# Softmax sums of a cross-attention block: from halves added by GpSimd to one VectorE reduction

## What is computed

```
q = (layernorm(x) @ Wq + bq)          # x: 8 x 1024 x 512, 16 heads of 32
k, v = ctx @ Wk + bk, ctx @ Wv + bv   # ctx: 8 x 64 x 384
attn = softmax(clip(q k^T / sqrt(32), -1e4, 1e4))    # over 64 keys
x = x + (attn @ v) @ Wo + bo
hidden = layernorm(x) @ W1 + b1       # 512 -> 2048
q = hidden + phase * w_imag * sin(theta + 0.1 hidden) * 0.1
out = x + relu(q) @ W2 + b2
```

## Time and profile before

| | |
|---|---|
| median of 3 runs | 1959.45 us (1958.43 to 1963.11) |
| the profiled execution | 1960.21 us, of which the traced span is 1958.1 us |
| TensorE matmul busy in the span | 1941.3 us, 99% |
| VectorE busy | 1486.9 us, 76% |
| ScalarE busy | 1263.7 us, 65% |
| GpSimd busy | 545.6 us, 28% |
| mean granted TensorE clock | 0.998 of full speed |

### The profile page before, as it was taken

One profiled execution on the slowest core, in us unless ns is written; L12 is line 12 of the kernel. 1 busy time (PEld: TensorE's weight loads), 2 busy tenths in 40 slices (PEclk: granted clock), 3 DMA queues, 4 the chain that ended last, 5 costly groups with the idle time before them and its releaser, 6 DMA issues.

```text
span 1958.1 us, 27917 instructions
## 1 busy us (share of the span) xinstructions
PE 1941.3 (99%) x9162; PEld 1624.4 (83%) x9162; DVE 1486.9 (76%) x2304; ACT 1263.7 (65%) x2132; POOL 545.6 (28%) x388
## 2 busy tenths in 40 slices
PE   9999999999999999999999999999999999999999
PEld 7788888888888878888888888888888888888887
DVE  8988888888875967787578768758757876875763
ACT  6767767667664867677377557647737755764761
POOL 7877777777773321000000000000000000000000
PEclk9999999999999999999999999999999999999999
DMA  7467687687675999889879888987987988897845
GB/s 243 145 185 185 172 209 179 172 214 190 169 157 161 339 323 336 277 271 290 275 264 270 265 280 252 286 289 238 290 272 266 270 267 279 252 286 245 250 151 193
DMA packets 363298, 472.75 MB, mean 241 GB/s; under 512 B 166032, under 2 KB 201872, under 8 KB 363152
## 3 DMA queue, kind: packets, MB, share of 16 engines
q1 hardware_dynamic: 346448, 439.44, 70.7%
q0 software_dynamic: 15840, 31.46, 9.4%
q10 hardware_dynamic: 864, 0.04, 0.0%
HBM read 347.90 MB, written 108.00 MB: 233 GB/s over the span
## 4 chain that ended last, share of the span: by engine, by line
PE 89%; DVE 4%; POOL 2%; DMA 2%; issue 2%; ACT 2%; SPq 0%; POOLq 0%; ACTq 0%; DVEq 0%
PE psum L1980 29%; PE psum L1982 29%; PE psum L1981 29%; PE psum L2073 2%; DMA stage<-in_w 1%; POOL prob L942 1%; PE psum L2022 0%; POOL prob L963 0%; DMA x_dram<-res 0%; DVE top L1617 0%; DMA acc<-in_w 0%; DVE prob L1608 0%; DVE stats L1481 0%; POOL q_lo L898 0%; DVE xt_lo L1717 0%
## 5 line engine op out<-in xcount | busy, mean ns | idle before, releaser
L1980 PE MATMUL psum<-w_ring,act_hi 128*128 128x512 f32 x1024 | 399.7, 390 | 3.6 <-DVE act_lo L1819 3.6
L1981 PE MATMUL psum<-w_ring,act_hi 128*128 128x512 f32 x1024 | 399.5, 390 | 0.0
L1982 PE MATMUL psum<-w_ring,act_lo 128*128 128x512 f32 x1024 | 399.5, 390 | 0.0
L1982 PE MATMUL psum<-xo,w_ring 128*128 128x512 f32 x784 | 305.1, 389 | 0.0
L1980 PE MATMUL psum<-xo,w_ring 128*128 128x512 f32 x784 | 305.1, 389 | 0.0
L1981 PE MATMUL psum<-xo,w_ring 128*128 128x512 f32 x784 | 305.1, 389 | 0.0
L1798 DVE SCALAR_TENSOR_TENSOR frac<-frac,turns 128x512 f32<-128x512 f32 x256 | 175.8, 696 | 77.3 <-ACT frac L1346 77.2
L1980 PEld LDWEIGHTS psum<-w_ring,act_hi 128*128 128x128 f32 x1024 | 192.8, 188 | 44.5 <-issue 4.4
L1982 PEld LDWEIGHTS psum<-w_ring,act_lo 128*128 128x128 f32 x1024 | 192.9, 188 | 40.1
L1981 PEld LDWEIGHTS psum<-w_ring,act_hi 128*128 128x128 f32 x1024 | 192.9, 188 | 39.9
L1383 ACT ACTIVATE frac<-frac 128x512 f32<-128x512 f32 x256 | 156.0, 626 | 104.4 <-DVE frac L1798 104.4
(11 more groups left out here) (186 smaller groups left out, 4341.1 us busy)
## 6 DMA issues: line engine op xcount, KB each, us to landing
w_ring<-w2s SPq DMA_DIRECT2D x240, 512.0 KB, 4.2
w_ring<-w1s SPq DMA_DIRECT2D x392, 256.0 KB, 4.2
x_sb<-turn_dram SPq DMA_DIRECT2D x58, 512.0 KB, 6.3
res<-in_x SPq DMA_DIRECT2D x64, 256.0 KB, 3.8
x_dram<-res SPq DMA_DIRECT2D x64, 256.0 KB, 3.1
x_dram<-bo_row POOLq DMA_DIRECT2D x16, 1024.0 KB, 11.0
acc<-x_dram SPq DMA_DIRECT2D x16, 1024.0 KB, 7.3
x_sb<-in_x SPq DMA_DIRECT2D x15, 1024.0 KB, 6.2
```

What stands on the lines that cost most here:

```text
L1980: pe.matmul(o, a_hi, b_hi, start=first, stop=False, skip_group_check=resumed)
L1981: pe.matmul(o, a_hi, b_lo, start=False, stop=False, skip_group_check=resumed)
L1982: return pe.matmul(o, a_lo, b_hi, start=False, stop=last, skip_group_check=resumed)
```

## The change

`total` of a group is now reduced by VectorE straight from the 64 exponentials of each head in `prob`: 128 partitions x 16 rows x 64 elements. Before, it reduced 128 x 16 x 32 elements of `halves`. GpSimd's addition that filled `halves` goes, with its two waits and its semaphore. VectorE waits for the exponential (`exp_done`) instead of the addition. The place of `sum_and_inverse` in each step's order is the same, as is all the rest.

```diff
             for i in range(GROUPS + 1):
-                if i:
-
-                    rows = prob[:, (i - 1) % SCORE_BUFS]
-                    pool.wait_ge(exp_done, i)
-                    if i >= 2:
-                        pool.wait_ge(total_done, i - 1)
-                    pool.tensor_tensor(halves[:], rows[:, :, 0:KEYS // 2], rows[:, :, KEYS // 2:KEYS], ALU.add)\
-                        .then_inc(halves_done, 1)
                 if i in V_LO_STEPS:
...
             def sum_and_inverse(i):
                 if 1 <= i <= GROUPS:
-                    dve.wait_ge(halves_done, i)
+                    dve.wait_ge(exp_done, i)
                     if i >= 3:
                         dve.wait_ge(prob_done, i - 2)
-                    dve.reduce_sum(total[:, (i - 1) % 2, :], halves[:], AX_X).then_inc(total_done, 1)
+                    dve.reduce_sum(total[:, (i - 1) % 2, :], prob[:, (i - 1) % SCORE_BUFS], AX_X).then_inc(total_done, 1)
```

More of the change, by code:

```diff
@@ L311, in xattn_ffn @@
         stats_raw, shift_rows_done = sem("stats_raw"), sem("shift_rows_done")
-        q_full_done, halves_done = sem("q_full_done"), sem("halves_done")
+        q_full_done = sem("q_full_done")
         xt_psum, xt_hi_done, xt_lo_done = sem("xt_psum"), sem("xt_hi_done"), sem("xt_lo_done")
```

## The result

The changed kernel takes 1963.88 us in the median of 20 runs (1961.0 to 1969.3), the kernel before 1960.55 us in the median of 20 runs beside it (1958.34 to 1963.11). The ratio is 1.0016, with a 95% interval of 1.0010 to 1.0022: 3.3 us or 0.16% slower, where 5.1 us were forecast. It lies within the 0.3% that the prediction calls no change, on the forecast side.

A forecast was written before the change was run, and what follows sets the result against it. TensorE was taken as the bound in settled attention, VectorE as pacing before about 97 us. Tiles +4.3, first tiles +1.5 and last groups -0.7 gave +5.1 us on 1959.45, about 1964.6 us; eight-in-ten range 1959.8 to 1969.0.

The forecast's parts named there:

- The place: Once per tile, a later `top` of group 29 delays `q_lo` of group 30 and TensorE, paid in full.
- Hidden everywhere: Rival: TensorE's prefetch and VectorE's idle time absorb the 0.38 us delay; about 1960.3 us, chance 0.12.
- The size of that term: Per settled tile, two longer sums less the vanished wait for `halves`: +0.38 us, in eleven tiles.
- Step 57: Its wait for `halves` is longer, 1.00 us, so the change costs only 0.1 us there.
- The first tiles: Up to 97 us VectorE sets the pace; longer sums, partly relieved, cost TensorE +1.5 us, bounds -0.5 to +2.9.
- `rstd`, which was queued behind it, moves into its place for 1.0: Beside the four early `xt_lo`, GpSimd's `rstd` replaces `halves` for 1.0 us, against the 1.3 us turn that goes.
- The end: Last groups: step 60's 1.84 us wait for `halves` and TensorE's stall behind it go; -0.7 us, bounds -0.9 to 0.
- The 0.2 us that steps 63 and 64 were to give back: In the last groups, steps 63 and 64 return about 0.2 us.
- a `tensor_reduce` does not contend: The longer VectorE sums do not hold back GpSimd; the opposite rule would cost 8 us more over 12 tiles.
- their slack at about 0.2 us: TensorE's transposes in each tile have about 0.2 us to spare before a delay reaches them.
- A second place per tile: Rival: slack at `q_lo` of group i = 3 or the transposes is eaten too; +11 us, about 1970.5, chance 0.11.
- GpSimd's freed time turns into longer waits: In settled tiles, removing 64 additions of 1.3 us or more only makes GpSimd wait longer for `inv` and `top`.

The follow-up runs named there:

- The extra reductions: Changed kernel plus one unused 128x512 VectorE reduction ahead of the sum in tile steps i = 1 (ratio 1.0053) or, in a second kernel, i = 3 (1.0022).
- the reduction in i = 1: Changed kernel plus one unused 128x512 VectorE reduction ahead of the sum in steps i = 1 of the tiles, 9 to 57: ratio 1.0053.

## Why the prediction was right, and where its terms were off

*The place.* One spot per tile, `q_lo` of the groups i = 2: right. Its load wait grew by 0.38, no other load of scores in the tile waited, and moving the sum out of that chain took the wait away. The extra reductions show that this chain passes on what is added to it, 0.58 of 0.6 us, and that the cover in step i = 3 is real, if nearly used up. "Hidden everywhere" is refuted by the lateness that grows by 0.32 us per tile and by the reduction in i = 1.

*The size of that term.* 2 x 0.54 - 0.70 = 0.38 per tile was forecast; the trace has 3.55 us over eleven tiles, 0.32. The sum lasts 1.20 to 1.21 us in the chain where I took 1.22, and so gained 0.53 rather than 0.54. At the scores of groups i = 2 themselves TensorE falls 0.36 us behind in the first seven tiles and 0.34 or less in the last four, where its wait before the change was already 0.24 to 0.26 rather than about 0.20. In the first seven it also wins back 0.03 at the next scores i = 1, which had come 9.17 us after those before them and now come 9.13 after. Step 57, forecast at +0.1, gained 0.09.

*The first tiles.* This term failed most: +1.5 forecast, +0.23 measured. The way up was right: scores 6 were 2.22 us later than before, 1.74 of it since the start, against 1.9 forecast. The step that failed is "`rstd`, which was queued behind it, moves into its place for 1.0". VectorE's four `xt_lo` took 4.79 us, 1.72 less than before, and a wait of 0.28 ahead of them went as well. The reciprocal of group 5 was 2.27 us late since the start (2.4 forecast), the clip of group 7 only 0.19: 2.1 us came back where 0.9 were forecast. `rstd` did not hold VectorE up at all: it ran from 87.19 to 88.64, and the third and fourth `xt_lo`, taken singly, started at 87.70 and 88.31 beside it and took 0.68 us each, their usual time. VectorE, then GpSimd in the changed kernel, beside the earlier trace rows:

```profile
84.20 4.79 DVE L1709 TENSOR_TENSOR xt_lo<-x_sb,xt_hi 128x512 fp32r<-128x512 f32 x4
```

```profile
84.88 2.35 POOL L942 TENSOR_TENSOR prob<-prob,inv 128x1024 f32<-128x1024 f32 x1
87.19 1.45 POOL L888 TENSOR_TENSOR rstd<-var_eps,minus_half 128x4 f32<-128x4 f32 x1
```

The kernel with the addition kept in step 7 alone shows how much of the relief is that addition: 1.08 us of the 1.5 by which the scores catch up between groups 6 and 9. The rest fits the additions of the other early steps, which cost 0.46 when they were kept.

*The end.* -0.7 forecast, -1.07 measured, with the mechanism as described. By the starts of matmuls the stall of 0.87 us before scores 61 goes to the last hundredth, and 0.09 at scores 59 (step 57) and 0.11 at scores 62 come with it: the sum in step 60 starts right behind `o_lo`, and the load of scores 61 waits for nothing, beside the earlier trace rows:

```profile
577.14 1.21 DVE L1589 TENSOR_REDUCE total<-prob 128x16 f32<-128x1024 f32 x1
```

```profile
584.61 0.19 PEld L1972 LDWEIGHTS psum<-kbd,q_hi 128*128 128x128 f32 x1
```

The 0.2 us that steps 63 and 64 were to give back did not appear: TensorE's last product with `wo` is 3.18 us later than before, as scores 63 were 3.19.

*The rivals.* The rule that the prediction took from the Trainium skill, page "SBUF — State Buffer", section "Who interferes with whom", that a `tensor_reduce` does not contend, held: GpSimd's shift and `q_lo`, which run beside sums, are nowhere longer than before. One scaling per tile did lengthen, in the seven steps i = 3 with a weight split: 2.36 us at 279.37, as shown above, where it was 1.90. VectorE's split (`w1a`, from 278.87) comes later behind the longer sum and now meets the scaling, where before it met `q_lo` (1.87 us at 276.15, now 1.29). The two nearly cancel, but this is the scaling that the transposes wait for. The forecast put their slack at about 0.2 us; for the groups i = 2 it was 0.04. "A second place per tile" did not come about in the changed kernel, but it was nearer than its chance of 0.11 says. With the addition kept in steps i = 3 it came, at these transposes. What kept it off was the removal of the addition, which I had costed at nothing in the settled part. "GpSimd's freed time turns into longer waits" is true of the additions outside steps i = 3 once the first tiles are over. It is not true of those beside `xt_lo`: with the longer sum, each of the twelve from step 11 to 55 would have cost 0.47 us.

## What to carry to other kernels

Before adding work to an engine with idle time, find which of its waits lies last ahead of the bound engine: the same 0.6 us cost 0.58 in one step of a tile and 0.03 in another. Work taken from an engine off the path is not worth nothing if another engine shares a resource with it; ask what its instructions would meet once the phases move by a tenth of a microsecond, not only what they meet now. A reordering that frees one chain should be checked against the next slack, at every wait of the bound engine and not only at the kind of wait that was freed (here 0.04 to 0.11 us, at transposes two steps away), and against what the moved instruction will then run beside. A load that waits need not delay the matmul behind it, so losses are read from the starts of matmuls.

## What the runs showed of the hardware

VectorE's subtraction with two operands in SBUF (128x512) and GpSimd's two-operand instructions of 128x512 and 128x1024 shut each other out for a whole instruction, in either direction, and arrival decides: with the addition 2.56 us behind the first `xt_lo` in both cases, 0.13 us in the end of the `q_lo` ahead turned a wait of GpSimd (1.76 us for 1.29) into one of VectorE (4.40 us for 3.17). The Trainium skill, page "SBUF — State Buffer", section "Who interferes with whom", has this as an exclusive lock, with the order of issue deciding who blocks; for these sizes the traces agree. GpSimd's `rstd` (two operands of 128x4, 1.03 us alone) is different: it waits for the `xt_lo` that it meets and ends 0.9 us behind that one's end, but the `xt_lo` that follow beside it keep their 0.68 us. The start of the first scores differed by up to 1.2 us between executions of kernels that do not differ there, and the two waits for the DMA of residual rows at the end of attention added up to between 2.9 and 5.7 us.
